# An attention and expert-path block on one core: score matmuls as 64-row tiles in pairs of heads, a shorter maximum pass, float32 steps gathered

## The reference, cut to what matters

```python
q, k, v = (split_heads(xn @ W.T) for W in (Wq, Wk, Wv))      # b, 16 heads, 1024, 16
q, k = _apply_rope(q, cos, sin), _apply_rope(k, cos, sin)
scores = jnp.einsum('bhqd,bhkd->bhqk', q, k) / jnp.sqrt(16.)
scores = jnp.where(causal, scores, -1e9)
probs = jax.nn.softmax(scores, axis=-1)
attn = jnp.einsum('bhqk,bhkd->bhqd', probs, v)
x_mixed = _mix(xn, mix_kernel)
h = jnp.einsum('bsd,pdm->bspm', x_mixed, W1) + b1
stacked = jnp.einsum('bspm,pmd->bspd', h, W2) + b2           # 9 paths
idx = argmax(tanh(x_mixed @ Wo1 + bo1) @ Wo2 + bo2)
out = x + attn @ Wo.T + layernorm(xn + stacked[idx], gamma, beta)
```

## Time and profile before

| what | us |
|---|---|
| median of 3 executions | 881.25 (878.26 to 882.08) |
| the profiled execution's own time | 879.47 |
| its span, first to last instruction | 877.7 |
| TensorE (PE) busy | 790.5 |
| VectorE (DVE) busy | 621.8 |
| ScalarE (ACT) busy | 458.2 |
| GpSimd (POOL) busy | 288.4 |
| mean granted TensorE clock | 0.971 of full speed |

### The profile page before, as it was taken

The page is one execution under the profiler, slowest core; times in us unless marked ns, Lnnn a source line. Parts: engine busy times, 40 slices in busy tenths (PEclk is TensorE's granted clock), DMA queues, the critical chain, the costliest instruction groups (busy, mean ns, idle before and its releaser), DMA issues.

```text
span 877.7 us, 12898 instructions
## 1 busy us (share of the span) xinstructions
PE 790.5 (90%) x4928; PEld 392.1 (45%) x4928; DVE 621.8 (71%) x1222; ACT 458.2 (52%) x780; POOL 288.4 (33%) x419
## 2 busy tenths in 40 slices
PE   4856979979999989989999998998999999999986
PEld 2522434344455534435455543434455554444434
DVE  5967796667678687567859679676867767766522
ACT  2452534645555644556546654564555564554662
POOL 1001032880515121583332402387051512120513
PEclk9967999999999999989999999999999999999999
DMA  6372323124421434021550623113441241410102
GB/s 216 108 180 47 75 49 53 36 64 123 69 51 31 95 97 73 1 73 64 108 98 1 115 79 76 27 37 100 109 78 21 49 97 30 73 29 1 25 1 72
DMA packets 40575, 59.99 MB, mean 68 GB/s; under 512 B 4813, under 2 KB 36830, under 8 KB 37634
## 3 DMA queue, kind: packets, MB, share of 16 engines
q1 hardware_dynamic: 36002, 54.39, 26.6%
q0 software_dynamic: 4224, 4.19, 3.2%
q10 hardware_dynamic: 288, 0.59, 0.2%
HBM read 42.04 MB, written 16.85 MB: 67 GB/s over the span
## 4 chain that ended last, share of the span: by engine, by line
PE 67%; DVE 19%; POOL 8%; ACT 2%; issue 2%; DMA 2%; SPq 1%; DVEq 0%; ACTq 0%; POOLq 0%
PE bank L1206 13%; PE bank L1187 11%; PE bank L1167 11%; PE bank L1153 8%; DVE piecemax L994 7%; PE bank L1143 5%; PE bank L1105 4%; PE bank L1234 3%; PE bank L1164 3%; PE bank L1116 2%; PE bank L1216 2%; PE bank L1123 2%; DVE stats L855 2%; POOL prob L671 2%; POOL turned L653 2%; POOL raw L654 2%
## 5 line engine op out<-in xcount | busy, mean ns | idle before, releaser
L994 DVE TENSOR_REDUCE piecemax<-bank 128x1 f32<-128x512 f32 (+3 forms) x608 | 380.7, 657 | 178.1 <-PE bank L1167 177.1
L778 ACT ACTIVATE prob<-bank 128x512 f32<-128x512 f32 x576 | 332.6, 596 | 317.6 <-PE bank L1187 313.9
L671 POOL TENSOR_SCALAR_AFFINE_SELECT prob<-prob 128x256 f32<-128x256 f32 (+1 forms) x320 | 132.5, 434 | 417.8 <-ACT prob L778 415.6
L1167 PE MATMUL bank<-k_st,q_st 96*128 96x128 bf16 (+3 forms) x1152 | 231.0, 281 | 11.9 <-DVE piecemax L994 11.7
L1187 PE MATMUL bank<-q_st,k_st 98*128 98x512 bf16 (+3 forms) x768 | 223.6, 333 | 13.9 <-DMA q_st<-shiftT 8.1
L1206 PE MATMUL bank<-prob,v_sb 128*17 128x512 f32 (+3 forms) x1536 | 158.7, 502 | 14.7 <-POOL prob L671 14.7
L1167 PEld LDWEIGHTS bank<-k_st,q_st 96*128 96x128 bf16 x1152 | 99.2, 100 | 146.2 <-issue 52.7
L1187 PEld LDWEIGHTS bank<-q_st,k_st 98*128 98x128 bf16 x768 | 71.5, 99 | 116.1 <-ACT prob L778 57.6
L1153 PE MATMUL bank<-w_sb,mid 128*128 128x256 f32 (+1 forms) x320 | 85.4, 390 | 2.2 <-DVE z L987 2.2
L1105 PE MATMUL bank<-xnT,wqk_sb 128*128 128x512 f32 x128 | 68.5, 637 | 5.2 <-ACT xnT L725 3.7
L1143 PE MATMUL bank<-xm,w_sb 128*128 128x512 f32 x128 | 67.5, 609 | 0.0
(11 more groups left out here) (82 smaller groups left out, 672.9 us busy)
## 6 DMA issues: line engine op xcount, KB each, us to landing
scratch<-parts SPq DMA_DIRECT2D x16, 768.0 KB, 3.8
q_st<-scratch SPq DMA_DIRECT2D x90, 128.0 KB, 6.9
k_st<-scratch SPq DMA_DIRECT2D x15, 384.0 KB, 4.8
z<-in_x SPq DMA_DIRECT2D x8, 512.0 KB, 4.6
mask<-chosen SPq DMA_DIRECT2D x16, 256.0 KB
z<-in_x POOLq DMA_DIRECT2D x8, 512.0 KB, 6.0
out<-z SPq DMA_DIRECT2D x8, 512.0 KB, 3.2
k_st<-scratch SPq DMA_DIRECT2D x15, 256.0 KB, 5.4
```

Of the source, the lines that this page charges most:

```text
L671: nc.gpsimd.affine_select(out=d, in_=d, compare_op=ALU.is_ge, fill=0.0, base=0, pattern=pattern, channel_multiplier=-1).then_inc(masked, 1)
L778: nc.scalar.activation(prob[:, place_of(G, i), :], ps[:, :], ACT.Exp, scale=float(DK) ** -0.5).then_inc(act_took, 1)
L994: nc.vector.tensor_reduce(piecemax[:, G % 2, t, h:h + len(cols), piece], ps[:, 0:len(cols) * w].rearrange("p (h k) -> p h k", k=w), AX.X, ...
L1167: ins = nc.tensor.matmul(ps[:, k * w:(k + 1) * w], q_st[0:PARTS, G % STACKS, h, t * P:(t + 1) * P], k_st[0:PARTS, G % STACKS, h, k0:k0 + w ...
```

## The change

**Tiles of 64 rows.** The stacks get 128 rows in two halves of 64: even heads in rows 0 to 63, odd heads in rows 64 to 127, each with two blocks in the free dimension. The first block (`LEAD`, 64 rows) has the four products of the leading parts, the second (`REST`, 32 rows, plus 2 for the shift) the other two. A score unit of an even head and one of an odd head are issued together: for each block one matmul in rows 0 to 63 into one bank and one in rows 64 to 127 into the other. Both banks must be free before the first of the four matmuls.

**The maximum pass** uses the first block alone, also in pairs. The units are cut anew (18 pairs, all banks full with 512 columns). The causal mask is now two matmuls of 64 rows a bank, of 512 and 256 columns, from `ident_rows` and `causal_sb`.

**Gathering.** `grouped()` takes every step other than S, sel, max, pv and osum out of the sorted list and puts it back, in its order, ahead of the next score unit whose number is 2 modulo 4.

**Fills** are 18 DMAs of 16 to 32 rows with two heads each, instead of 9 with four. `place_shift` is 2 DMAs as before. `req` shares memory with `score_sb`.

```diff
-PARTS = 6 * DK
+LEAD = 4 * DK
+REST = 2 * DK
-PIECES = 3
-Q_PARTS = (0, 0, 0, 1, 1, 2)
-K_PARTS = (0, 1, 2, 0, 1, 0)
+PIECES = 4
+PAIRS = GH // 2
+ROW = P // 2
+Q_PARTS = ((0, 1, 0, 1), (0, 2))
+K_PARTS = ((0, 1, 1, 0), (2, 0))
+FILL_DMAS = 2 * sum(len(runs(parts)) for parts in Q_PARTS + K_PARTS)
...
-            add(G + i / NS, "S", G, i)
+            add(G + (i - i % 2) / NS, "S", G, i)
...
-        a, e = (0, 0.22) if G == 0 else (G - 0.75, G + 0.02) if G == 1 else (G - 0.95, G + 0.03)
+        a, e = (0, 0.22) if G == 0 else (G - 0.72, G + 0.0) if G == 1 else (G - 1, G + 0.0)
         for u in units:
-            at = a + (e - a) * (u - units[0]) / len(units)
+            at = a + (e - a) * (u // 2 - units[0] // 2 + 0.99) / (len(units) // 2)
...
-    return [(at, name) for at, _, name in items]
+    return grouped([(at, name) for at, _, name in items])
+
+def grouped(items):
+    out, later = [], []
+    for at, name in items:
+        if at >= 0 and name[0] not in ("S", "sel", "max", "pv", "osum"):
+            later.append((at, name))
+            continue
+        if name[0] == "S" and name[2] % 4 == 2:
+            out += later
+            later = []
+        out.append((at, name))
+    return out + later
...
-                st = k_st[:, G % STACKS, :, a:e]
-                for row, first, rows in ((0, 0, 3 * DK), (3 * DK, 0, 2 * DK), (5 * DK, 0, DK)):
-                    eng.dma_start(st[row:row + rows], src[1][first:first + rows]).then_inc(done, 16)
-                st = q_st[:, G % STACKS, :, a:e]
-                for k, part in enumerate(Q_PARTS):
-                    eng.dma_start(st[k * DK:(k + 1) * DK], src[0][part * DK:(part + 1) * DK]).then_inc(done, 16)
+                for st, parts, qk in ((k_st, K_PARTS, 1), (q_st, Q_PARTS, 0)):
+                    for odd in range(2):
+                        for k in range(2):
+                            for row, first, count in runs(parts[k]):
+                                r, w = odd * ROW + row, count * DK
+                                eng.dma_start(st[r:r + w, G % STACKS, :, k, a:e],
+                                              src[qk][first * DK:first * DK + w, odd::2, :]).then_inc(done, 16)
...
-                ps = begin(("max", G, u))
-                if piece == 0:
-                    nc.tensor.matmul(ps[:, :].rearrange("p (h k) -> p h k", h=GH), ident_bf[:, :],
-                                     causal_sb[:, None, :].to_broadcast([P, GH, P]), start=True, stop=False)
...
+                ps = [begin(("max", G, u - 1)), begin(("max", G, u))]
+                rows = [slice(odd * ROW, (odd + 1) * ROW) for odd in range(2)]
+                causal = piece == 0
+                if causal:
+                    for m in range(2):
+                        for odd in range(2):
+                            nc.tensor.matmul(
+                                ps[odd][:, :].rearrange("p (c k) -> p c k", k=P)[:, :, m * ROW:P],
+                                ident_rows[rows[odd], int(m != odd), :],
+                                causal_sb[rows[odd], None, 0:P - m * ROW].to_broadcast([ROW, HALF // P, P - m * ROW]),
+                                start=(m == 0), stop=False)
...
-                ps = begin(("S", G, i))
...
+                ps = [begin(("S", G, i - 1)), begin(("S", G, i))]
...
+                    for part, rows in ((0, LEAD), (1, REST + SHIFT)):
+                        for odd in range(2):
+                            h, r = SCORE_UNITS[i - 1 + odd][2][x][0], odd * ROW
+                            ins = nc.tensor.matmul(ps[odd][:, c:c + w],
+                                                   k_st[r:r + rows, k, h // 2, part, kb * P:(kb + 1) * P],
+                                                   q_st[r:r + rows, k, h // 2, part, q:q + w],
+                                                   start=(part == 0), stop=(part == 1))
```

More of the change, by code:

```diff
@@ L37, with runs, unit @@
 STACKS = 3
-PIECES = 3
-Q_PARTS = (0, 0, 0, 1, 1, 2)
-K_PARTS = (0, 1, 2, 0, 1, 0)
+PIECES = 4
[3 more added lines that the diff above has]
+K_PARTS = ((0, 1, 1, 0), (2, 0))
+def runs(parts):
+    out = []
+    for k, a in enumerate(parts):
+        if out and out[-1][1] + out[-1][2] == a:
+            out[-1][2] += 1
+        else:
+            out.append([k * DK, a, 1])
+    return out
+FILL_DMAS = 2 * sum(len(runs(parts)) for parts in Q_PARTS + K_PARTS)
 def max_units():
     out = []
-    for t in range(NT):
-        out.append((t, 0, [(h, t * P, P) for h in range(GH)]))
-        for piece, k0, w in ((1, 0, min(t, HT) * P), (2, HALF, (t - HT) * P)):
-            if w > 0:
-                n = 4 if w == P else 2 if w == 2 * P else 1
-                out += [(t, piece, [(h, k0, w) for h in range(a, a + n)]) for a in range(0, GH, n)]
+    def unit(tiles, pairs, piece, w, first):
+        out.append((tiles, pairs, piece, w, [(t, p, first(t)) for t in tiles for p in pairs]))
+    both = range(PAIRS)
+    for half in range(2):
+        a = half * HT
+        for t in (a, a + 2):
+            unit(range(t, t + 2), both, 0, P, lambda t: t * P)
+        if half:
+            for t in range(a, NT):
+                for p in both:
+                    unit(range(t, t + 1), range(p, p + 1), 1, HALF, lambda t: 0)
+        for t in (a + 2, a + 3):
+            unit(range(t, t + 1), both, 2, 2 * P, lambda t: half * HALF)
+        unit(range(a + 1, a + 4, 2), both, 3, P, lambda t: (t - 1) * P)
     return out
@@ L118 @@
 PARTS_OF = {"qk": 2, "v": 2, "early": 2, "mid": 2, "paths": 5, "proj": 2}
-FIRST_UNITS = [u for u in range(NM) if MAX_UNITS[u][0] < HT]
+FIRST_UNITS = [u for u in range(NM) if MAX_UNITS[u // 2][0][0] < HT]
+assert all(SCORE_UNITS[i][2][0][0] % 2 == i % 2 for i in range(NS))
 def prologue():
@@ L486, in build @@
         NCONSTS = 4
-        FILL_DMAS = 9
         def unit(name):
@@ L990, in max_unit @@
             def max_unit(G, u):
-                t, piece, cols = MAX_UNITS[u]
+                tiles, pairs, piece, w, cols = MAX_UNITS[u // 2]
                 ps = take(("max", G, u))
-                h, _, w = cols[0]
-                nc.vector.tensor_reduce(piecemax[:, G % 2, t, h:h + len(cols), piece],
-                                        ps[:, 0:len(cols) * w].rearrange("p (h k) -> p h k", k=w),
-                                        AX.X, ALU.max).then_inc(dve_took, 1)
+                nc.vector.tensor_reduce(
+                    piecemax[:, G % 2, tiles.start:tiles.stop:tiles.step, u % 2, pairs.start:pairs.stop, piece],
+                    ps[:, 0:len(cols) * w].rearrange("p (t h k) -> p t h k", t=len(tiles), k=w),
+                    AX.X, ALU.max).then_inc(dve_took, 1)
             def cut_shift(G, half):
@@ new lines, in max_scores @@
+                for c, (t, p, k0) in enumerate(cols):
+                    last = c == len(cols) - 1
+                    for odd in range(2):
+                        ins = nc.tensor.matmul(ps[odd][:, c * w:(c + 1) * w],
+                                               q_st[rows[odd], k, p, 0, t * P:(t + 1) * P],
+                                               k_st[rows[odd], k, p, 0, k0:k0 + w],
+                                               start=not causal, stop=(last or not causal))
+                        if last:
+                            ins.then_inc(slot_filled, 1)
@@ L1259, in _ @@
                 elif what == "S":
-                    score(*name[1:])
+                    if name[2] % 2:
+                        score(*name[1:])
                 elif what == "pv":
```

95 lines of the change are left out of this document (53 added, 42 removed).

## The result

| | before | changed |
|---|---|---|
| median of the executions, us | 881.25 | 1055.37 |
| ratio, 95% interval | | 1.198 (1.196 to 1.200) |

The change makes the kernel slower by 20%, 174 us. The forecast was slower, 956 us, in a range of 885 to 1010; the range missed the time by 45 us.

What follows compares the result with a forecast made beforehand. TensorE's queue was taken to set the time. From the profile's 879.5 us, -70 + 23 + 112 + 49 + 5 + 6 - 50 = +75 gave 954.5, stated as 956 us, range 885 to 1010.

Steps and rivals of the forecast that it cites:

- Rival B: VectorE runs ahead, its cut is done before TensorE's turn, other waits vanish: 867 us, or 832; chance 0.12.
- Fewer columns: TensorE's maximum pass and mask stream 320 banks less at 0.22 us each: -70 us.
- rivals C and D: Row tiles on TensorE: C, three quarters of full overlap, 1010 us, 0.08 with rival E; D, no overlap, 1150, 0.03.
- Changes of tile: TensorE switches between row tiles, column groups and whole array 244 more times at 0.095 us: +23 us.
- Score pairs: TensorE waits for ScalarE to free both score banks, mainly in 86 short gaps at 1.09 us: +112 us.
- Turned shift: TensorE's turn of the shift waits for VectorE's cut and steps gathered ahead of it: 54 us against 5.3, +49.
- GpSimd: Masks still stand behind rotations gathered ahead of diagonal score units, between 0 and 10 us more: +5 us.
- The start: With 18 first-fill DMAs, the store and second fill come later and delay the first score unit's shift: +6 us.
- Given back: Waits TensorE had anyway disappear where it now stands still, between 17 and 98 us: -50 us.
- rival A: Stalls in every pair lower TensorE's granted clock, so streaming takes 6% more: 990 us; chance 0.17.
- rival E: Maximum pair takes two of three banks, emptying by VectorE may bind; folded into upper side; 0.08 together with C.

Runs made afterwards that it cites:

- 64-row matmuls: Kernel before plus one extra 8-column matmul of 64 rows ahead of every second score unit: 914.47 us; the control with 96 rows: 884.63 us.
- balanced order: Changed kernel with the gathered steps put ahead of score units 0, 6, 10, 16, 20, 24, 28 and 32 instead of 2 modulo 4: 1061.36 us.
- whole-array pairs alone: Kernel before with score units issued two at a time, both banks waited for first, no row tiles and no gathering: 894.57 us.

## Why the prediction was right and wrong

**Right: the direction and, in the main, its mechanism.** That TensorE's queue sets the time, that the pairs' double wait and the gathered cut would hold it, and that waits outweigh the shorter maximum pass, is what the trace shows. Rival B (the gathered work is covered) had its own test in the sentence on what would prove me wrong, waits at the score line below 40 us; they were 99.9.

**The terms.** Fewer columns: -70 forecast, -67 in the starts of the matmuls. The row tiles overlap fully, and my rivals C and D fall; the Trainium skill ("TensorE: Matmul & The Clock Gate", Part 3, Measured speedup) has 3.07 of 4 for four tiles, which two tiles at 512 columns do not show here. Changes of tile: +23 forecast for 244; in the starts of the matmuls 260 more with 25 us, and another 13 us of first float32 weights that I had not seen. With the 64-row matmuls, 52 us of such gaps made 30 us of time. Score pairs: +112 forecast, 99.9 us of waits against 5.0, though the restart is 0.15 us and not a few hundredths. Turned shift: +49 forecast, 44.8 less 5.3. GpSimd: +5 forecast, the wait fell by 13 us. The start: the first score unit began 7.2 us later against 6 forecast; the 18 issues end at 45.30, the stores follow, and the shift stands behind the second fill:

```profile
37.00 4.55 SPq L607 DMA_DIRECT2D k_st<-scratch  x10
41.59 3.71 SPq L607 DMA_DIRECT2D q_st<-scratch  x8
45.35 1.01 SPq L587 DMA_DIRECT2D scratch<-parts  x2
...
57.91 3.71 SPq L607 DMA_DIRECT2D q_st<-scratch  x8
61.66 1.47 SPq L615 DMA_DIRECT2D q_st<-shiftT  x2
...
64.39 1.04 PE L1266 MATMUL bank<-q_st,k_st 64*128 64x512 bf16 x4 [7.82 <-DMA q_st<-shiftT]
```

**Wrong: the step "Given back", -50.** I let the other waits of TensorE disappear in the new stalls. They grew. Without the score line's and the shift's, the view's rows are 96 us against 71: +25 where I had -50, 75 us of the miss. The small gaps below the view's rows did not shrink either: gaps less waits and changes of tile are about 50 us before and 60 now. The rows that grew most are the maximum line (27.9 against 11.7) and the second layer of the paths (13.1 against 2.2), both behind VectorE, and the gathered kernel without any row tile has the same two, 27.9 and 12.0. Stalls of TensorE would give slack to engines that run freely. Here each engine walks the same gathered list, and while TensorE waits for one result, the engine that owes the next one can be waiting as well. The trace shows such a chain, with ScalarE, VectorE and TensorE (line 806 is a step gathered with others on ScalarE's queue, L974 is its producer on VectorE):

```profile
201.95 1.98 DVE L974 TENSOR_TENSOR turned<-turned,parts 128x1024 f32<-128x1024 f32 x1
...
203.97 1.04 ACT L806 CAST parts<-turned 128x1024 bf16<-128x1024 f32 x1 [1.58 <-DVE turned L974]
204.92 1.08 ACT L837 ACTIVATE prob<-bank 128x512 f32<-128x512 f32 x2
...
205.05 1.33 DVE L979 TENSOR_TENSOR parts<-turned,parts 128x1024 bf16<-128x1024 f32 x1 [1.11 <-ACT parts L806]
...
206.14 0.62 PE L1266 MATMUL bank<-q_st,k_st 64*128 64x384 bf16 x8 [2.74 <-ACT prob L837]
206.31 1.28 DVE L1052 TENSOR_REDUCE piecemax<-bank 128x2 f32<-128x512 f32 x2
...
208.21 0.61 PE L1238 MATMUL bank<-k_st,q_st 64*128 64x256 bf16 x4
...
208.75 3.23 PE L1165 MATMUL bank<-xnT,wqk_sb 128*128 128x512 f32 x4
```

VectorE's subtraction is gathered; ScalarE's cast stands right behind it, waits 1.58 us for it, and holds back two exponentials whose scores were ready; TensorE waits 2.74 us for these. Meanwhile VectorE's next step (L979) waits 1.11 us for the same cast, and its two maxima, whose scores were ready too, start only at 206.31. ScalarE's waits at L806 are 17.2 us in 11 times, 10.4 in the gathered kernel before, and 5.0 in 10 times before. This is one chain; how much of the 75 us such chains make is not shown. My count took account of the gaps between score pairs on TensorE and of VectorE's queue ahead of the cut, not of the short chains that gathering lines up on ScalarE.

**Wrong: rival A kept apart.** The slower clock was a rival with a price of 37 us, but it isn't an alternative to the waits; it comes along with them and belonged in the sum. The last row above is its face: right after TensorE's stall, four projection passes take 3.23 us at 208.75, where four of the same line took 1.99 at 430.91. The windows view of these two stretches (PE, PEld, DVE, ACT, POOL, clock, DMA) has the granted clock:

```profile
200.00:208.20 8.20, 5.13 (x38) 1.70 (x34) 5.72 (x6) 5.21 (x9) 8.12 (x11) 0.98 0.10 36
208.20:212.00 3.80, 3.80 (x14) 1.39 (x12) 1.29 (x2) 1.14 (x2) 0.76 (x2) 0.59 0.39 134
```

From 0.98 it falls to 0.59, mostly the level of 1.2 GHz, after 5.1 of 8.2 us busy. Over the kernel that is 40 to 50 us. The gathered kernel before, with no row tile, lost 45 us against 19 in the same way, so it does not need row tiles. No run changed the clock alone: that the stalls bring it down is read from the order of events in such stretches.

Put together for the profiled execution, with each stretch of TensorE's time counted once: 954.5, +75 for the given back, -17 for the score pairs (94.9 more than before, for 112), -10 for the shift, -11 for GpSimd and the start, whose waits are in the 75 already, +51 for the clock, +2 and +13 for changes of tile and first weights, +3 for the columns. That is 1061, against 1069 measured; 8 us are open. It tells where the time stands, not what would come back if one item were removed.

**Wrong as an argument: terms that add.** The balanced order removed 75 us of waits at the score line and gained nothing. My 112 us was near the true size of a wait (99.9), and no price of it. And the gathering alone, without pairs, costs 87 us, with only 20 of it at the two lines to which I had put its cost. The Trainium skill ("TensorEngine Tiling (Array Packing)", PSUM Bottleneck) warns that emptying PSUM may take over; I had put it aside (rival E) because VectorE had room on average. It has, 58% busy in the balanced order, and still the maximum line waited 114 times there, where 121 of the stretches between maximum pairs held less than 0.5 us of TensorE work, against 59 in the changed kernel.

What stays open: how the 57 us that row tiles and their units cost in the gathered order split between changes of tile, the two banks that a maximum pair wants at once and the shorter cover. Only the first was measured by itself.

## What to carry to other kernels

When a step is made to need two buffers at once, count ahead of it, gap by gap in the order, how much other work the engine has until both are free; the mean says nothing, and here 86 of 287 gaps had 0.2 us where 1.4 were needed. When such a wait is removed, look at what it had been pacing, before claiming its length as a gain. And gathering steps by kind to save switches of 0.1 us lines up producers with consumers on every engine that walks the list: a switch saved was worth 0.05 us here, and the gathering cost 87 to 124 us.

## What the runs showed of the hardware that was not expected

- Two row tiles of 64 rows overlap without loss at 512 columns: pairs start a median of 4 ns apart, a pass takes 0.216 us (0.220 for the whole array before), and two passes of four matmuls take 0.45 us.
- A change between whole array, row tiles and column groups leaves a gap of 0.09 to 0.11 us (medians) in every direction measured; the Trainium skill ("TensorEngine Tiling (Array Packing)", Key Properties) says such a change drains the engine, and the trace agrees. After a change to the whole array a first float32 pass takes 0.53 us instead of 0.43, and its weight load starts with it and not ahead of it.
- Where TensorE waits for both banks of a pair, it restarts 0.144 us (median) after the second exponential, in the changed kernel (107 waits) and with whole-array pairs alone (36 waits). Before, with one bank, 11 of 20 restarts took 0.055 us, most others 0.12 to 0.16.
- The mean granted clock is lower in the kernels whose TensorE stands still in many short stretches: 0.96 to 0.97 before, 0.93 to 0.94 with the gathering alone, 0.91 to 0.93 with the change.
